# Two heads' contexts in the same 128 rows, reciprocals turned instead of contexts, and a new order on three engines

## What is computed

```python
h = attention(emb[x])              # 16 heads of 16 features, softmax over 128 keys, Wo, bo
n = layernorm(h)
h = h + sigmoid(n @ gate_w.T + gate_b) * exclusive_scan(decay, (n @ B_w.T) @ C_w.T)
h = h + layernorm(h) @ sign(weight).T
```

## Time and profile before

| | |
|---|---|
| median of 3 runs | 740.04 us (739.85 to 740.42) |
| profiled execution | 740.43 us, span of the records 738.7 us |
| TensorE matmul busy | 690.1 us, 93% of the span |
| ScalarE busy | 577.4 us, 78% |
| VectorE busy | 518.6 us, 70% |
| GpSimd busy | 376.9 us, 51% |

### The profile page before, as it was taken

The page is one execution under the profiler, slowest core; times in us unless marked ns, Lnnn a source line. Parts: engine busy times, 40 slices in busy tenths (PEclk is TensorE's granted clock), DMA queues, the critical chain, the costliest instruction groups (busy, mean ns, idle before and its releaser), DMA issues. The chain is left out here.

```text
span 738.7 us, 21201 instructions
## 1 busy us (share of the span) xinstructions
PE 690.1 (93%) x7047; PEld 649.1 (88%) x7047; DVE 518.6 (70%) x1147; ACT 577.4 (78%) x1643; POOL 376.9 (51%) x431
## 2 busy tenths in 40 slices
PE   4589999999999999999999999999999999999862
PEld 3478999999999999999999999999999999998762
DVE  3656777778777777777777777787777777877532
ACT  2488888888888888888888888888888888888510
POOL 7402354555556545455465555554555555544553
PEclk9799999999999999999999999999999999999986
DMA  5422233332223333332333333322233333221000
GB/s 142 112 91 90 97 115 104 113 112 93 81 87 101 114 111 102 113 102 69 89 95 114 114 99 114 104 77 86 87 114 114 99 114 106 87 82 69 16 15 28
DMA packets 56016, 69.68 MB, mean 94 GB/s; under 512 B 6768, under 2 KB 41648, under 8 KB 55984
## 3 DMA queue, kind: packets, MB, share of 16 engines
q1 hardware_dynamic: 52048, 60.48, 24.1%
q0 software_dynamic: 3072, 8.39, 6.7%
q10 hardware_dynamic: 864, 0.40, 0.2%
HBM read 10.52 MB, written 8.39 MB: 26 GB/s over the span
## 5 line engine op out<-in xcount | busy, mean ns | idle before, releaser
L372 ACT ACTIVATE probs<-ps_s,neg_max 128x128 f32<-128x128 f32 x1024 | 295.5, 383 | 74.9 <-DVE neg_max L518 74.9
L518 DVE TENSOR_REDUCE neg_max<-ps_s 128x4 f32<-128x512 f32 x256 | 175.9, 688 | 96.9 <-PE ps_s L641 93.8
L294 POOL TENSOR_TENSOR xn<-h,mv 128x512 f32<-128x512 f32 x64 | 66.7, 1042 | 216.5 <-DVE ve L545 216.5
L381 ACT COPY probsT<-ps_t 128x512 f32<-128x512 f32 x256 | 157.6, 615 | 15.0 <-PE ps_t L717 11.3
L717 PE MATMUL ps_t<-ident,probs 128*128 128x128 f32 x1024 | 154.3, 273 | 6.5 <-ACT probsT L381 6.2
L717 PEld LDWEIGHTS ps_t<-ident,probs 128*128 128x128 f32 x1024 | 119.9, 141 | 13.0 <-issue 5.1
L641 PE MATMUL ps_s<-k_stack,q_stack 128*128 128x256 f32 x512 | 123.7, 323 | 3.9 <-DMA q_stack<-q_low 3.9
L641 PEld LDWEIGHTS ps_s<-k_stack,q_stack 128*128 128x128 f32 x512 | 77.7, 192 | 4.3 <-DMA q_stack<-q_low 4.3
L287 POOL DMA_INDIRECT x_emb<-in_emb,id_col x64 | 64.8, 1013 | 23.2 <-issue 14.1
L307 POOL TENSOR_TENSOR state_high<-state_in,ones_col 128x512 fp32r<-128x512 f32 x32 | 33.2, 1037 | 81.3 <-DVE state_in L630 81.3
L533 DVE BATCH_NORM_STATS2 stats<-h 128x6 f32<-128x256 f32 x128 | 48.2, 418 | 33.9 <-POOL h L319 32.8
(11 more groups left out here) (126 smaller groups left out, 1877.3 us busy)
## 6 DMA issues: line engine op xcount, KB each, us to landing
k_stack<-k_high SPq DMA_DIRECT2D x128, 128.0 KB
q_stack<-q_high SPq DMA_DIRECT2D x64, 256.0 KB
k_stack<-k_low SPq DMA_DIRECT2D x64, 128.0 KB
q_stack<-q_low SPq DMA_DIRECT2D x32, 256.0 KB
out<-y SPq DMA_DIRECT2D x32, 256.0 KB, 2.1
x_emb<-in_emb,id_col POOLq DMA_INDIRECT x64, 3.8
raw<-in_wkT SPq DMA_DIRECT2D x1, 256.0 KB, 3.4
raw<-in_wqT SPq DMA_DIRECT2D x1, 256.0 KB, 4.5
```

What stands on the lines that cost most here:

```text
L294: nc.gpsimd.tensor_tensor(xn[:], h[:], mv[:, :, 0:1].to_broadcast([P, 2, D]), ALU.subtract).then_inc(centred, 1)
L372: last = nc.scalar.activation(probs[s % 2][:, j], ps_s[s % 2][:, j * SEQ:j * SEQ + SEQ], ACT.Exp, bias=neg_max[s % 2][:, j:j + 1])
L381: nc.scalar.copy(probsT[st][:], ps_t[:]).then_inc(act_pT, 1)
L518: nc.vector.tensor_reduce(neg_max[s % 2][:], ps_s[s % 2][:].rearrange("p (h k) -> p h k", h=HPS), axis=AX.X, op=ALU.max, negate=True).then ...
```

## The change

* Contexts: the stationary operand of a head is still 32 columns, but now 16 of v and 16 of zeros, taken from `v_wide` at an offset such that head i fills the first 16 of 32 rows and head i + 8, accumulated into the same rows, the last 16. Both sequences' contexts, feature-major, fill the one bank `ps_c`. The rows of Wo are put in the matching order on the host side (`ctx_order`), and there is no column of ones.
* Row sums: for steps 0, 1, 2, 6, 7 each Exp pass of ScalarE also gives the sum of its results (`accum_out`), 20 of 32 passes a pair; for steps 3, 4, 5 VectorE sums the probabilities in one pass a step (`sums`).
* Reciprocals: one pass of VectorE (`invert_sums`), widened to 16 columns a head by one pass of GpSimd, turned by four transposes of TensorE into g2 (`invert_rows`), copied by ScalarE (`move_inverse`), and multiplied into `ps_c` by VectorE (`normalise_context`). Its result `ctx_feat` is split by ScalarE (`move_ctx`) and VectorE, each from SBUF.
* Gone are `context_rows`, the contexts' `to_features`, both copies of `ctx_raw`, both `context_norm`.
* Order: on TensorE the transposes of x stand after step 0 instead of 1, those of xn2 after step 7 instead of 6, those of the reciprocals after step 4. On VectorE the second layernorm's statistics stand after maxima 4 instead of 3 and its moments after q_low in step 5 instead of 4; k_low and xn1Tl stand together after maxima 3, xTl after maxima 1, xn2Tl ahead of state_in. On GpSimd the widening stands between the two layernorms' work. ScalarE's exponentials 5 to 7 wait for the sums of the step two before them, whose buffer they overwrite.

```diff
+HALF = HEADS // 2
+VROW = HD + HALF * VW
+SUMMED = (3, 4, 5)
...
-        v_aug = [sb(f"v_aug{p}", [P, 2, HEADS, VW]) for p in range(2)]
+        v_wide = [sb(f"v_wide{p}", [P, 2, 2, VROW]) for p in range(2)]
+        row_sum = [sb(f"row_sum{p}", [P, 2, HEADS]) for p in range(2)]
...
-        inv_sum = sb("inv_sum", [P, 2, HEADS])
-        ctx_tok = sb("ctx_tok", [P, 2, D])
+        inv_sum, inv_wide = sb("inv_sum", [P, 2, HALF, 2]), sb("inv_wide", [P, 2 * HEADS, HD])
+        inv_rows, ctx_feat = sb("inv_rows", [P, C * 2 * SEQ]), sb("ctx_feat", [P, C, 2, SEQ])
...
+                if exists(t - 1):
+                    await_event(pool, dve_inv, 1, t - 1, 1)
+                    await_event(pool, pe_inv, 1, t - 2, 1)
+                    nc.gpsimd.tensor_tensor(
+                        inv_wide[:], inv_sum[:].rearrange("p b i a -> p (b i a)").unsqueeze(2).to_broadcast([P, 2 * HEADS, HD]),
+                        ones_col[:, 0:1].unsqueeze(1).to_broadcast([P, 2 * HEADS, HD]), ALU.mult).then_inc(pool_inv, 1)
...
+            for b in range(2):
+                act.dma_start(bv_rows[:, b], bv.partition_broadcast(P)).then_inc(small_loaded, 16)
...
+                        if s - 2 in SUMMED:
+                            await_event(act, dve_sum, len(SUMMED), t, s - 2 - SUMMED[0] + 1)
                         for j in range(HPS):
+                            at = s % 4 * HPS + j
+                            taken = None if s in SUMMED else row_sum[par][:, s // 4, at:at + 1]
                             last = nc.scalar.activation(probs[s % 2][:, j], ps_s[s % 2][:, j * SEQ:j * SEQ + SEQ],
-                                                        ACT.Exp, bias=neg_max[s % 2][:, j:j + 1])
+                                                        ACT.Exp, bias=neg_max[s % 2][:, j:j + 1], accum_out=taken)
                         last.then_inc(act_exp, 1)
                 def move_probsT(s):
                     pair, st = before(t, s, 2)
                     if exists(pair):
                         await_event(act, pe_pT, STEPS, pair, st + 1)
-                        await_event(act, pe_pv, STEPS, pair - 1, st + 1)
+                        await_event(act, pe_pv, 2, pair - 1, st // 4 + 1)
                         nc.scalar.copy(probsT[st][:], ps_t[:]).then_inc(act_pT, 1)
-                def move_ctx(pair, b):
...
+                        await_event(act, pe_inv, 1, pair, 1)
+                        await_event(act, dve_ctx, 1, pair - 1, 1)
+                        nc.scalar.copy(inv_rows[:], g2[:]).then_inc(act_inv, 1)
+                def move_ctx(pair):
+                    if exists(pair):
+                        await_event(act, dve_ctx, 1, pair, 1)
+                        await_event(act, pe_o, 1, pair - 1, 1)
+                        nc.scalar.copy(ctxT[0][:], ctx_feat[:]).then_inc(act_ctxT, 1)
...
+                move_block(t + 1, xT[0], g3, pe_x, pe_v, act_x)
                 move_probsT(1)
                 exponentials(1)
-                move_block(t + 1, xT[0], g3, pe_x, pe_v, act_x)
                 move_probsT(2)
-                move_ctx(t - 1, 1)
...
                 move_probsT(4)
+                move_inverse(t - 1)
                 exponentials(4)
...
+                move_ctx(t - 1)
                 move_probsT(6)
-                move_block(t - 1, ctxT[0], g2, pe_ctxT, pe_o, act_ctxT)
-                move_ctx(t, 0)
...
-                def context_norm(b, block):
...
+                def sums(s):
+                    if exists(t):
+                        await_event(dve, act_exp, STEPS, t, s + 1)
+                        nc.vector.tensor_reduce(row_sum[par][:, s // 4, s % 4 * HPS:s % 4 * HPS + HPS], probs[s % 2][:],
+                                                axis=AX.X, op=ALU.add).then_inc(dve_sum, 1)
+                def invert_sums():
                     if exists(t - 1):
+                        await_event(dve, act_exp, STEPS, t - 1, STEPS)
+                        await_event(dve, dve_sum, len(SUMMED), t - 1, len(SUMMED))
+                        await_event(dve, pool_inv, 1, t - 2, 1)
+                        nc.vector.reciprocal(inv_sum[:].rearrange("p b i a -> p b a i"),
+                                             row_sum[1 - par][:].rearrange("p b (a i) -> p b a i", a=2)).then_inc(dve_inv, 1)
+                def normalise_context():
+                    if exists(t - 1):
+                        await_event(dve, pe_pv, 2, t - 1, 2)
+                        await_event(dve, act_inv, 1, t - 1, 1)
+                        await_event(dve, dve_ctxlo, 1, t - 2, 1)
+                        nc.vector.tensor_tensor(ctx_feat[:].rearrange("p c b s -> p (c b s)"), ps_c[:], inv_rows[:],
                                                 ALU.mult).then_inc(dve_ctx, 1)
...
                 maxima(1)
                 if exists(t - 2):
                     norm_moments(stats1, mv1, ve1, dve_mv1, dve_ve1, t - 2)
-                context_norm(0, g1)
+                invert_sums()
+                low_features(t + 1, xT, g3, act_x, pe_v, dve_xlo)
                 maxima(2)
                 if exists(t):
                     await_event(dve, pe_v, 1, t, 1)
-                    await_event(dve, pe_pv, STEPS, t - 2, STEPS)
+                    await_event(dve, pe_pv, 2, t - 2, 2)
                     nc.vector.tensor_tensor(
...
+                        v_wide[par][:, :, :, HD:VROW].rearrange("p b a (i w) -> p (b a) i w", w=VW)[:, :, :, 0:HD],
+                        g2[:].rearrange("p (n i w) -> p n i w", n=4, w=HD),
+                        bv_rows[:].rearrange("p b (a i w) -> p (b a) i w", a=2, w=HD),
                         ALU.add).then_inc(dve_v, 1)
-                low_features(t + 1, xT, g3, act_x, pe_v, dve_xlo)
...
                                                    ALU.mult).then_inc(dve_gated, 1)
                 maxima(3)
+                if exists(t + 1):
+                    split_low(k_low, g1, bk_col, k_high, act_khi, dve_klo)
+                low_features(t - 2, xn1T, g3, act_xn1T, pe_state, dve_xn1lo)
+                maxima(4)
                 if exists(t - 3):
                     norm_stats(t - 3, h1, pool_h1, stats2, dve_st2)
+                sums(3)
                 if exists(t - 3):
                     await_stats(t - 3, dve_st2, pool_xn2)
-                context_norm(1, g2)
+                maxima(5)
+                normalise_context()
                 if exists(t + 1):
-                    split_low(k_low, g1, bk_col, k_high, act_khi, dve_klo)
-                maxima(4)
-                low_features(t - 2, xn1T, g3, act_xn1T, pe_state, dve_xn1lo)
+                    split_low(q_low, g0, bq_col, q_high, act_qhi, dve_qlo)
                 if exists(t - 3):
                     norm_moments(stats2, mv2, ve2, dve_mv2, dve_ve2, t - 3)
-                maxima(5)
-                if exists(t + 1):
-                    split_low(q_low, g0, bq_col, q_high, act_qhi, dve_qlo)
+                sums(4)
                 maxima(6)
-                low_features(t - 1, ctxT, g2, act_ctxT, pe_o, dve_ctxlo)
+                sums(5)
+                if exists(t - 1):
+                    await_event(dve, act_ctxT, 1, t - 1, 1)
+                    await_event(dve, pe_o, 1, t - 2, 1)
+                    nc.vector.tensor_tensor(ctxT[1][:], ctx_feat[:], ctxT[0][:].bitcast(fp32),
+                                            ALU.subtract).then_inc(dve_ctxlo, 1)
                 maxima(7)
+                low_features(t - 3, xn2T, g3, act_xn2T, pe_ffn, dve_xn2lo)
                 if exists(t - 2):
...
                                             ALU.mult).then_inc(dve_in, 1)
-                low_features(t - 3, xn2T, g3, act_xn2T, pe_ffn, dve_xn2lo)
...
-                    for back in (6, 5, 4, 3):
...
-                def context_rows(b, dst):
...
+                    pair, st = before(t, s, 3)
+                    if not exists(pair):
+                        return
+                    vp = par if s >= 3 else 1 - par
+                    b = st // 4
+                    await_event(pe, act_pT, STEPS, pair, st + 1)
+                    if b == 0:
+                        await_event(pe, dve_v, 1, pair, 1)
+                        await_event(pe, dve_ctx, 1, pair - 1, 1)
+                    for c in range(C):
+                        at = slice((2 * c + b) * SEQ, (2 * c + b + 1) * SEQ)
+                        for a in range(2):
+                            for j in range(4):
+                                i = 4 * c + j
+                                head = HALF * a + i
+                                values = v_wide[vp][:, b, a, HD - HD * a + VW * i:HD - HD * a + VW * i + VW]
+                                last = mm(ps_c[VW * j:VW * j + VW, at], values,
+                                          probsT[head // HPS + 4 * b][:, head % HPS], a == 0, a == 1)
+                    last.then_inc(pe_pv, 1)
+                def invert_rows(dst):
```

(37 more changed lines are left out.)

58 lines of the change are left out of this document (12 added, 46 removed).

## The result

The changed kernel takes **834.47 us** (median of 4 runs, 833.54 to 836.5) against 740.23 us for the kernel before on the same chip (739.85 to 740.56): a ratio of 1.127, 95% interval 1.125 to 1.129. It is 94 us slower; 11 us faster had been forecast, and the range ended at 748. The same kernel on another chip took 834.60 us beside 740.63, so the loss is not that of one chip.

The account below looks back on a forecast made before the run. TensorE, 93% busy, was taken to bound the kernel. Gains of 29 x (0.87 - 0.60) = 7.8, 0.87 in turn 2 and 2.0 in turn 32, together 10.7 us, gave 729.3 us from 740.04; range 711 to 748.

Parts of the forecast that it names:

- Other waits, costed at nothing: Context(6), h1 behind the reciprocals' pass, and the copy of ps_t behind xTh: taken as covered, 0 us.
- xn2's wait: TensorE's transposes of xn2 wait for GpSimd's multiply, because the second layernorm's moments come later: 0.60 us a turn.
- the walk: Moments, GpSimd, xn2 followed on the old turn's clock: xn2's transposes wanted at 311.37, possible at 311.97.
- VectorE and GpSimd in each other's way: Rival, chance 0.16: the contexts' low part, two inputs in SBUF, blocks GpSimd's xn2 multiply by 0.57 us; 746 us.
- The natural turn: TensorE's turn without new waits: 21.02 less 0.87 us for two fewer sets of transposes, 20.15 us.
- The accumulation into the same rows: Context matmuls: the second head accumulating into the first's rows costs 0; the rival that it is not free had 0.04.
- The accumulator output: ScalarE's Exp passes: 0.08 us for each of 20 outputs; the rival that it is dear had 0.16.
- The number of TensorE's instructions: TensorE: three sets of four transposes a pair become one, context matmuls stay 32 a pair.
- ffn is covered: TensorE's ffn: its inputs are ready at 314.5, TensorE comes at 314.63, so covered by 0.1 us.
- Turns 0 and 1: Start of the kernel, short of ScalarE: what it loses and gains nearly cancels, 0 within 2 us either way.

Follow-up runs that it names:

- e8: Kernel before with only the x transposes in step 0 and xTh ahead of the copy of ps_t: 785.43 us, ratio 1.060 in the second run.
- e2: Changed kernel with TensorE's x transposes back in step 1, behind the v product: 800.48 us.
- e7: Changed kernel with the contexts' low part computed from bank g2 instead of ctx_feat, which gives it another value: 826.70 us.
- e4: Changed kernel with both x-path moves undone, second layernorm's statistics again behind maxima 3 and moments behind maxima 4: 760.85 us, ratio 1.027.
- e9: e6 with the second layernorm's statistics behind maxima 4 and its moments directly behind maxima 5, ahead of the context multiply: 733.73 us, ratio 0.991.
- e11: e9 with VectorE's sums(3) moved from behind maxima 4 to directly behind maxima 3: 726.92 us, ratio 0.980.
- e1: Changed kernel with ScalarE's cast xTh back behind exponentials 1: 815.42 us, ratio 1.099.
- e6: Changed kernel's dense contexts and turned reciprocals alone, everything else in the old order: 745.56 us, ratio 1.006 in the second run.

## Why the prediction was wrong, step by step

**The step that failed** is "Other waits, costed at nothing": "The copy xTh now delays the copy of `ps_t` by 0.48 in step 1; [...] it is done about when TensorE wants to turn step 2." I charged the move with the length of the moved instruction and not with its wait. xTh waits until the v product of its own turn has ended (311.56), and the copy behind it inherits this wait: 1.25 us idle on TensorE, 1.41 from start to start. In the kernel before it did not show, because xTh stood behind the exponentials and came when v was done anyhow. The wait is in the code: the fifth argument of `move_block` is what frees the destination. e8 shows it without the rest of the change: the two moves of the x path cost 44.5 us.

**A step that was missing.** The x transposes' move on TensorE was not costed at all, nor was the gather that feeds them, though xn2, which I myself had walked to a later place, stands ahead of the gathers in GpSimd's queue. It costs 1.34 us a turn (24.17 to 22.83, e2). The two errors together are the x path's 47.6 us.

**xn2's wait: right in place, forecast at half its size.** TensorE loses 1.18 us instead of 0.60. Of the missing 0.58, 0.31 is the contention of the rival (from the start of `ve` at 300.50 to the multiply's end at 303.94 it is 3.44 us, forecast 3.13; e7: 0.28 a turn). The other 0.27 can be read from the last matmul of the k product, in the walk and in the changed kernel:

```profile
301.68 0.28 PE L641 MATMUL ps_g<-xTh,wkl 128*128 128x256 f32 x1
```

```profile
293.30 0.28 PE L685 MATMUL ps_g<-xTh,wkl 128*128 128x256 f32 x1
300.50 0.17 DVE L569 TENSOR_SCALAR ve<-mv 128x2 f32<-128x2 f32 x1
```

TensorE wants xn2 9.52 us after it (302.82), where the walk has 9.69 (311.37): 0.17 earlier. `ve` starts 7.20 after it, in the walk 7.12 (308.80): 0.08 later. The last 0.02 is the handover to TensorE. The 0.17 comes from the turn that was walked: the turns of the kernel before alternate between about 21.15 and 20.90 us, and from the transposes of xn1 to those of xn2 it takes 8.90 us in the turn walked (302.23 to 311.13) and 8.72 in the one before it (281.35 to 290.07). Taking the moves of the second layernorm back was worth 1.06 us a turn (e4); e9, with the statistics behind maxima 4 and only the moments earlier, has no wait for xn2 either, so the moments' place is what matters.

**VectorE and GpSimd in each other's way.** The mechanism is as described. I had the multiply wait for the 0.57 us that would be left of VectorE's pass; in the trace 0.45 us was left (303.04 less 302.59), and the multiply starts no later, but its row is 0.31 longer. It is so in every turn. At the end of the pipeline, where the passes meet in another way, the order is the other one: GpSimd first, VectorE's low part second. First the changed kernel, then e11:

```profile
794.63 1.04 POOL L303 TENSOR_TENSOR xn<-h,mv 128x512 f32<-128x512 f32 x1 [2.01 <-DVE ve L569]
794.88 1.33 DVE L667 TENSOR_TENSOR ctxTl<-ctx_feat,ctxTh 128x512 fp32r<-128x512 f32 x1 [0.33 <-ACT ctxTh L414]
795.63 1.15 POOL L305 TENSOR_TENSOR rs<-ve,neg_half 128x2 f32<-128x2 f32 x1
```

```profile
673.99 1.04 POOL L308 TENSOR_TENSOR xn<-xn,rs 128x512 f32<-128x512 f32 x1
674.40 1.18 DVE L667 TENSOR_TENSOR ctxTl<-ctx_feat,ctxTh 128x512 fp32r<-128x512 f32 x1
```

Here GpSimd keeps its 1.04, and VectorE's pass of 0.68 grows by 0.65 with 0.79 left of the other, and by 0.50 with 0.63 left. GpSimd's power behind it, 0.70 elsewhere, then grows by 0.45 with 0.58 left of VectorE's pass. In all four cases the one that starts second gets longer, by what is left of the first less 0.13 or 0.14 us. This trace bears out the rule of the Trainium skill ("SBUF — State Buffer", Who interferes with whom) that the two contend for a shared pair of SBUF ports, which one of them holds at a time, the first to issue ahead of the other; the wait lies within its own row. The forecast of this rival, 746 us, was no better than mine, since both lacked the x path.

**The parts that held.** The natural turn: 20.15 forecast; e11 has 20.46 x 397.11 / 400 = 20.31 us of busy TensorE, so TensorE's work fell by 0.70 us a turn (21.01 to 20.31), where 0.87 was forecast. The accumulation into the same rows was free: the 32 records of the contexts take 1.01 us to the next start (313.57 to 314.58), as before. The accumulator output: 0.08 forecast; in the trace an Exp pass starts 0.345 us after the last one with it (306.12 less 305.87 for the pass, 0.09 for its read), 0.25 without, so 0.09 to 0.10. The number of TensorE's instructions held too. That ffn is covered held in the changed kernel only, where TensorE itself is late by its other waits; in e4, without them, ffn waits 0.46 us a turn.

**The ends.** Turns 0 and 1 were put at 0, within 2, and this failed too. The first state_in multiply, in turn 2, starts at 82.9 us before, at 89.3 in the changed kernel and at 87.2 in e11: the start costs 6.4 and 4.3 us. TensorE's waits for copies of `ps_t` from 40 to 90 us, 4.5 us before, 8.3 and 7.2 after, are a part of it; the rest was not looked into. From the first state_in to the last it is 636.9 us before, 726.7 in the changed kernel (89.8 more) and 619.5 in e11 (17.4 less).

**Why single repairs gave less than their wait.** ScalarE and VectorE hand lateness on. e1 took away 1.41, and the turn fell by 0.65; of the 1.18 lost at xn2, the last wait of the turn, 1.06 came away, and ffn's wait came in its place. What remains open is which of the parts of e9's edit (statistics later, moments between maxima 5 and the multiply) has how much of the 11.8 us; they weren't tried one by one.

## What to carry to other kernels

When an instruction is moved ahead in an in-order queue, charge the move with the latest thing that it waits for, buffer releases among them, and follow everything behind it to the bottleneck engine; its own length is the small part. A reserve between a producer and a consumer (here 3.5 us between a gather's landing and the transposes) is to be written down before either is moved, since two harmless moves can spend it twice. And when a structural saving comes with a new order, run it first in the old order, and then look for the waits that the new work itself has made: here the old order alone stood 5 us above the kernel before (e6), two more edits made from its waits (e9, e11) gave 14 us below it, and the order that came with the change cost 108 us against that.
